# Adjacency build of a graph network: node groups of 17 in place of 16, their first edges counted exactly

## The chip, the cores and the metric

The kernel runs on one core of one Trainium2 chip. The metric is device time in microseconds (us) of one execution. TensorE is called PE in the profile, VectorE DVE, ScalarE ACT, GpSimd POOL, and SyncE, which here only issues transfers, SP.

## The reference, cut to what matters

Four graph layers run one after the other on 3,125 nodes with 96 features. All use the same 100,000 directed edges, whose `dst` is sorted:

```
_o = jnp.argsort(dst, stable=True)
src = src[_o]
dst = dst[_o]
...
msgs = xs[src]
agg = jax.ops.segment_sum(msgs, dst, num_segments=n_nodes)
...
x = x + _L0_gnn_ref(...)   # graph convolution, twice, batch norm between
x = x + _L1_gnn_ref(...)   # mean aggregation, twice
x = x + _L2_gnn_ref(...)   # attention over edges and self loops, twice
x = x + _L3_gnn_ref(...)   # normalized sum over edges
```

Every layer is preceded by a layer norm and a ReLU. The kernel gathers nothing edge by edge. It first builds the dense matrix of edge counts, source node by destination node, in 16 bit floats, and each `segment_sum` is then a matrix product with it.

## The kernel before

`build_adjacency` (L156) makes the matrix `adjacency` (`k.ADJ`). Its 3,125 destination columns are split into `NW` = 196 groups of `W` = 16 nodes. A source node is a row (`src & 127`, one of 128 partitions) and a tile (one of `NT` = 25). The edges of a group are a window of `WE` = 640 consecutive edges, that is `WT` = 5 batches of 128. A batch becomes two one-hot matrices: `hot_row` (edge by source row) and `hot_code` (edge by destination node within the group and source tile, a "code" out of 25 x 16 = 400). Their product on PE, summed over the five batches in PSUM (`counts`), is the group's part of the matrix. Since `dst` is sorted, batch b of a window holds only some of the group's nodes, and `RANGES` says which, so that the one-hot codes of a batch are narrower than 400. An edge that none of the ranges or windows reaches is found at the end by the total of the counts, and a slow loop over everything then runs (`sp.If(again)` and its like).

Four groups are a quad, and there are 49 quads. For each quad (`hot`, L349), DVE makes `hot_row` of all five batches with one instruction (L354) and `hot_code` of batches 0 to 3 with four instructions (L361). ACT makes the code of batch 4 out of a distance and a ReLU (L582, L590). PE multiplies (`pair`, L475: two groups, 16 matmuls, L486; three pairs of PSUM banks rotate), and ACT copies the counts of each pair into `adjacency` (L604). A matmul pair on each stored pair sums the out-degrees (L496).

Windows are loaded in eight loads (`LOADS`) of 4 to 36 groups, one transfer of two rows (`edge_keys`: row and code of each edge) per group, from an address that a register holds (L147, L152). SP issues nearly all of them, ACT a few of the first three loads. PE transposes a load's keys (`turn`, L470), and DVE unpacks them (`unpack`, L340, L341, L346).

The start addresses come first. Before the change, DVE takes every 25th edge of `dst` (32 samples in each of 125 partitions, L309, L311), compares each sample's group with all 196 group numbers (`below`, four instructions of 1,568 elements, L322), and PE sums the results over partitions and samples (32 matmuls of 196 columns, L456). 25 times the count (L330) is an address at most 25 edges ahead of the group's first edge. Five `bn_stats` of the first layer norm (L331) stand before L330, 20 behind it. Between the comparisons stands other work that the keys need: row and tile of each source (L313, L314), `dst_scaled` by ACT (L553) and the code (L317). SP and ACT write both keys to DRAM (L257, L558). The window transfers wait for those writes and for L330.

PE also runs matmuls whose results nobody reads, `keep_busy` (L449): 60 before the counting and 45 behind it, each `NW` columns wide. They stand in PE's queue ahead of the first `turn`.

The order of work on each engine is the order in which the code is written. Engines wait for each other by semaphores.

Of the kernel before, what the change touches and what calls it, by code (L numbers as in the profile page):

```python
# [13 lines left out]
I32 = mybir.dt.int32  # L14
# [18 lines left out]
W = 16  # L33
# [3 lines left out]
STEP = 25  # L37
NS = EF // STEP
SLICES = 4
LEAD = STEP  # L40
KEYS = LEAD + E + WE
CODES = NT * W
HALF = 0.5
RANGES = ((0, 6), (2, 10), (5, 15), (9, 16), (12, 16))
# [3 lines left out]
          for (lo, hi), seen in zip(RANGES, (0, 6, 10, 15, 16))]  # L48
QUAD = 4
ADDRESSES = 12  # L50
LOADS = (4, 8, 16, 24, 36, 36, 36, 36)
# [6 lines left out]
STATS_FIRST = 5  # L58
# [84 lines left out]
def load_windows(nc, k, d, eng, engine, load, keys, windows, landed):  # L143

    for at in range(0, len(windows), ADDRESSES):
        some = windows[at:at + ADDRESSES]
        _, starts = nc.values_load_multi_w_load_instructions(  # L147
            k.start_i[0:1, some[0]:some[-1] + 1], engines=[engine], min_val=0, max_val=STEP * EP * NS,
            skip_runtime_bounds_check_because="a start is STEP times a count of at most EP * NS samples")
        for w, start in zip(some, starts):  # L150
            i = w - FIRST[load]
            eng.dma_start(keys[2 * i:2 * i + 2, load % 2, :], d.keys[:, bass.ds(start, WE)]).then_inc(landed, 16)  # L152


def build_adjacency(nc, k, d, c):

    def sb(name, shape, dt):
        return c.enter_context(nc.sbuf_tensor(name, shape, dt))
# [20 lines left out]
    sample_i = sb("sample_i", [P, NS], I32)  # L179
    sample = sb("sample", [P, NS, 2], F16)  # L180
# [9 lines left out]
    below = [k.ADJ[0:EP, 7 + s, 0:NS // SLICES * NW] for s in range(SLICES)]  # L190
    pads = k.ADJ[0:1, 7 + SLICES, 0:4 * (LEAD + WE)].bitcast(F32).rearrange("p (e n) -> p e n", e=2)
# [14 lines left out]
    stats_ready = sem("stats_ready")  # L206
# [11 lines left out]
    key_writes = 16 * 6  # L218
# [24 lines left out]
    @block.sync  # L243
    def _(sp):
        for part, array in zip((dst[0:EVEN, :], dst[EVEN:EP, :]), pieces(d.dst)):
            sp.dma_start(part, array).then_inc(dst_in, 16)
        sp.wait_ge(pads_ready, 3)
        sp.dma_start(d.keys[:, 0:LEAD], pads[:, :, 0:LEAD]).then_inc(keys_out, 16)
        sp.dma_start(d.keys[:, LEAD + E:KEYS], pads[:, :, LEAD:LEAD + WE]).then_inc(keys_out, 16)
# [6 lines left out]
        for part, array in zip((code_f[0:EVEN, :], code_f[EVEN:EP, :]), pieces(d.keys[1, LEAD:LEAD + E])):  # L256
# [12 lines left out]
        again = sp.value_load(missed, min_val=0, max_val=1)  # L269
        with sp.If(again):  # L270
            sp.dma_start(g_row_f, d.keys[0, LEAD:LEAD + E].rearrange("(p f) -> p f", p=EP)).then_inc(g_keys_in, 16)
            sp.dma_start(g_code, d.keys[1, LEAD:LEAD + E].rearrange("(p f) -> p f", p=EP)).then_inc(g_keys_in, 16)
            sp.wait_ge(g_keys_in, 32)

    @block.gpsimd
    def _(pool):
# [6 lines left out]
        pool.iota(own[:, :], pattern=[[CODES // 2 * QUAD, MOST // QUAD], [0, WT], [CODES // 2, QUAD]], base=0,  # L283
# [10 lines left out]
        pool.memset(zeros[:, :], 0.0).then_inc(idents, 1)  # L294

    @block.vector
    def _(dve):
# [3 lines left out]
        dve.memset(pads[:, 1, 0:LEAD], -1.0).then_inc(pads_ready, 1)  # L301
        dve.memset(pads[:, 1, LEAD:], HALF * NT * (N + P)).then_inc(pads_ready, 1)
# [6 lines left out]
        chain(dve.tensor_scalar(sample_i[0:EP, :], dst.rearrange("p (s j) -> p s j", j=STEP)[:, :, 0], 4, None,  # L309
                                ALU.logical_shift_right))  # L310
        chain(dve.tensor_copy(sample[0:EP, :, :], sample_i[0:EP, :].unsqueeze(2).to_broadcast([EP, NS, 2])))  # L311
# [6 lines left out]
                                       op1=ALU.add).then_inc(codes_ready, 1)  # L318
        dve.wait_ge(iotas, 1)
        n = NS // SLICES  # L320
        for s in range(SLICES):
            dve.tensor_tensor(below[s].rearrange("p (s a b) -> p s a b", s=n, b=2),  # L322
                              bound[0:EP, :].rearrange("p (a b) -> p a b", b=2).unsqueeze(1).to_broadcast([EP, n, NW // 2, 2]),
                              sample[0:EP, s * n:(s + 1) * n, :].unsqueeze(2).to_broadcast([EP, n, NW // 2, 2]),
                              ALU.is_gt).then_inc(below_ready, 1)
        dve.wait_ge(x_in, 16 * (NG + 1))
        for t in range(NT):
            if t == STATS_FIRST:
                dve.wait_ge(count_ready, 1)
                dve.tensor_scalar(k.start_i[:, :], count_ps, float(STEP), None, ALU.mult).then_inc(starts_ready, 1)  # L330
            last = dve.bn_stats(node_stats[:, t, :], k.X[:, t, :])  # L331
        last.then_inc(stats_ready, 1)
        dve.wait_ge(iotas, 4)

# [14 lines left out]
        def hot(load, q):  # L349
# [94 lines left out]
    def _(pe):  # L444
        n = NS // SLICES
# [102 lines left out]
    def _(act):  # L548
# [8 lines left out]
        for part, array in zip((row_f[0:EVEN, :], row_f[EVEN:EP, :]), pieces(d.keys[0, LEAD:LEAD + E])):  # L557
            act.dma_start(array, part).then_inc(keys_out, 16)  # L558
# [16 lines left out]
        def distances(load, q):  # L575
# [4 lines left out]
            for w in range(QUAD):  # L580
                at = (q - quads(load)[0]) * QUAD + w
                nc.scalar.activation(distance[:, q % 2, w, :], codes_iota[:, FROM[-1]:CODES], ACT.Abs,  # L582
                                     bias=negative[:, load % 2, at:at + 1]).then_inc(distance_ready, 1)
# [1738 lines left out]
```

## Time and profile before

| | |
|---|---|
| time, median of 3 runs | 815.18 us (814.97 to 815.38) |
| span of the profiled execution, first to last instruction | 812.5 us |
| mean granted clock of PE | 0.953 of full |
| PE busy | 737.1 us (91%) |
| DVE busy | 605.8 us (75%) |
| ACT busy | 462.9 us (57%) |

No separate time of the profiled execution is given beyond its span. The median lies 2.7 us above the span, which is what lies around the first and last instruction. Shares of busy time are averages over stages with different limits. The adjacency build takes about the first 191 us, and only its rows bear on the change.

### The profile page before, as it was taken

The page shows a single profiled execution, that of the slowest core. Times are in us where ns is not written, and L with a number is a line of the kernel's source. Part 1 is how long each engine was busy: PE and PEld are TensorE (multiplying, and loading weights), DVE is VectorE, ACT ScalarE, POOL GpSimd, SP SyncE. Part 2 cuts the span into 40 slices and gives each one's busy share as a digit, 9 for nine tenths or more (in the row PEclk, how much of TensorE's full clock was granted, in tenths as well). Part 3 has the DMA queues.
Part 4 walks back from the last instruction along what each step waited for, and adds up shares of the span by engine and source line. Part 5 has one row for each costly group of instructions (what it writes and reads, how often), then busy time and mean ns, then how long its engine had stood idle before and what let it go on. Part 6 is the DMA issues. An engine that isn't in the chain of part 4 may idle for free. (4 is left out here: it accounts for less than half of the span.)

```text
span 812.5 us, 21039 instructions
## 1 busy us (share of the span) xinstructions
PE 737.1 (91%) x8477; PEld 681.0 (84%) x8477; DVE 605.8 (75%) x1376; ACT 462.9 (57%) x911; POOL 4.8 (1%) x15
## 2 busy tenths in 40 slices
PE   7888888888997999999999849999964999997997
PEld 6656666657997999999999839999964999997997
DVE  7999999997437445543444589999978999996732
ACT  2898898894004023212123668999656899973600
POOL 2000000000000000000000000000000000000000
PEclk9999999999999999999999979999965999998999
DMA  5000000001994000000000410776651099997801
GB/s 143 13 12 12 13 7 1 2 2 19 411 414 191 2 1 2 2 2 2 2 14 26 127 35 18 227 228 211 213 183 62 18 181 216 206 203 190 177 26 36
DMA packets 121660, 78.13 MB, mean 96 GB/s; under 512 B 98088, under 2 KB 116058, under 8 KB 121432
## 3 DMA queue, kind: packets, MB, share of 16 engines
q1 hardware_dynamic: 121216, 75.89, 33.2%
q8 instruction: 70, 1.15, 0.6%
q10 hardware_dynamic: 344, 0.85, 0.3%
q14 instruction: 30, 0.25, 0.1%
HBM read 30.46 MB, written 25.79 MB: 69 GB/s over the span
## 5 line engine op out<-in xcount | busy, mean ns | idle before, releaser
L1888 PE MATMUL banks<-loose,adjacency 128*128 128x194 f16 x1250 | 212.4, 247 | 0.0
L663 PE MATMUL banks<-y_sb,adjacency 128*128 128x192 f16 (+1 forms) x1875 | 165.9, 248 | 1.3 <-DVE h_sb L910 1.1
L663 PEld LDWEIGHTS banks<-y_sb,adjacency 128*128 128x128 f16 x1875 | 161.2, 99 | 2.2 <-DVE h_sb L910 1.3
L486 PEld LDWEIGHTS counts<-hot_code,hot_row 128*128 128x128 f16 x1568 | 92.8, 101 | 61.8 <-DVE hot_code L361 35.8
L1887 PE MATMUL banks<-x_sb,gat_masks 128*128 128x194 f16 x820 | 141.4, 248 | 1.9 <-DVE adjacency L1802 1.9
L486 PE MATMUL counts<-hot_code,hot_row 128*128 128x100 f16 (+3 forms) x1568 | 122.5, 218 | 20.0 <-DVE hot_code L361 14.9
L1858 ACT ACTIVATE gat_masks<-y_sb,node_scalars 128x640 bf16<-128x640 f32 x164 | 121.9, 827 | 4.0 <-PEq L117 4.0
L1888 PEld LDWEIGHTS banks<-loose,adjacency 128*128 128x128 f16 x1250 | 122.6, 98 | 0.3
L361 DVE TENSOR_TENSOR hot_code<-codes_iota,unpacked 128x600 f16<-128x600 f16 x196 | 96.8, 554 | 0.0
L604 ACT ACTIVATE adjacency<-counts 128x800 f16<-128x800 f32 x98 | 81.5, 832 | 18.0 <-PE counts L486 18.0
L1887 PEld LDWEIGHTS banks<-x_sb,gat_masks 128*128 128x128 f16 x820 | 80.4, 98 | 3.1 <-DVE y_sb L1798 2.4
L354 DVE TENSOR_TENSOR hot_row<-rows_iota,unpacked 128x2560 f16<-128x2560 f16 x49 | 72.5, 1479 | 0.0
L1141 ACT ACTIVATE y_sb<-banks 96x256 f32<-96x256 f32 x50 | 19.1, 382 | 93.6 <-PE banks L1173 93.6
L1798 DVE TENSOR_TENSOR gat_masks<-gat_masks,adjacency 128x1920 f16<-128x1920 bf16 (+1 forms) x64 | 64.2, 1005 | 6.7 <-ACT gat_masks L1858 6.4
L582 ACT ACTIVATE distance<-codes_iota,negative 128x100 f16<-128x100 f16 x196 | 57.6, 370 | 13.3 <-DVE negative L346 13.3
L1802 DVE TENSOR_TENSOR adjacency<-adjacency,gat_masks 128x1920 f16<-128x1920 f16 (+1 forms) x64 | 63.9, 1006 | 0.4
L692 DVE TENSOR_REDUCE h_sb<-banks 128x96 f32<-128x192 f32 x50 | 17.8, 356 | 57.0 <-PE banks L663 56.4
L692 DVE TENSOR_REDUCE y_sb<-banks 128x96 f32<-128x192 f32 x50 | 17.7, 355 | 52.5 <-PE banks L663 52.5
L663 PE MATMUL banks<-loose,adjacency 128*128 128x192 f16 x625 | 55.7, 246 | 0.0
L663 PEld LDWEIGHTS banks<-loose,adjacency 128*128 128x128 f16 x625 | 52.7, 99 | 0.0
L2160 PE MATMUL banks<-y_sb,adjacency 128*128 128x192 f16 x625 | 52.3, 245 | 0.2 <-DVE y_sb L2080 0.2
L2160 PEld LDWEIGHTS banks<-y_sb,adjacency 128*128 128x128 f16 x625 | 52.1, 97 | 0.3 <-issue 0.3
(236 smaller groups left out, 1008.4 us busy)
## 6 DMA issues: line engine op xcount, KB each, us to landing
kept_adj<-adjacency SPq DMA_DIRECT2D x5, 4000.0 KB, 30.4
adjacency<-kept_adj SPq DMA_DIRECT2D x25, 800.0 KB, 9.0
y_sb<-a_dst_rows SPq DMA_DIRECT2D x10, 320.0 KB, 4.0
window_keys<-edge_keys SPq DMA_DIRECT2D x187, 5.0 KB
residual<-h_sb SPq DMA_DIRECT2D x5, 240.0 KB, 2.0
kept_x<-x_sb SPq DMA_DIRECT2D x1, 1200.0 KB, 5.2
loose<-residual SPq DMA_DIRECT2D x5, 240.0 KB, 3.6
x_sb<-kept_x SPq DMA_DIRECT2D x5, 240.0 KB, 4.9
```

Of the source, the lines that this page charges most:

```text
L354: dve.tensor_tensor(hot_row[:, h, :, :].rearrange("p n (a b) -> p n a b", b=2), rows_iota[:, :].rearrange("p (a b) -> p a b", b=2).unsquee ...
L361: dve.tensor_tensor(hot_codes(h, b).rearrange("p w (a b) -> p w a b", b=2), codes_iota[:, FROM[b]:FROM[b] + WIDE[b]].rearrange("p (a b) -> ...
L486: last = nc.tensor.matmul(counts[:, 2 * (p % HELD) + i, start:end], hot_row[:, q % 2, b * QUAD + w, :], hot_codes(q % 2, b)[:, w, start - ...
L582: nc.scalar.activation(distance[:, q % 2, w, :], codes_iota[:, FROM[-1]:CODES], ACT.Abs, bias=negative[:, load % 2, at:at + 1]).then_inc(d ...
L604: nc.scalar.activation(k.ADJ[:, :, 2 * p * W:2 * (p + 1) * W].rearrange("p t (b o) -> p t b o", o=W), counts_of(2 * (p % HELD), 2), ACT.Co ...
L663: return nc.tensor.matmul(k.ps[:, j % G, 0:cols], k.ADJ[:, i, j * P:(j + 1) * P], y[:, i, 0:cols], start=i == 0, stop=i == NT - 1)
L1798: dve.tensor_tensor(masks(u, F16), masks(u, mybir.dt.bfloat16), counts_of(u), ALU.min).then_inc(t.over_ready, 1)
L1802: dve.tensor_tensor(counts_of(u), counts_of(u), masks(u, F16), ALU.subtract).then_inc(t.under_ready, 1)
L1858: nc.scalar.activation(step_of(x), row[ch % 2], ACT.Relu, bias=k.a_s5[:, i:i + 1], scale=STEEP).then_inc(t.step_ready, 1)
L1887: nc.tensor.matmul(bank[:, 0:2 * BC], over_of(x)[:, q * P:(q + 1) * P], features[0][:, i, :], start=i == 0, stop=False)
L1888: return nc.tensor.matmul(bank[:, 2 * BC:4 * BC], under_of(x)[:, q * P:(q + 1) * P], features[1][:, i, :], start=False, stop=i == NT - 1)
L2160: return nc.tensor.matmul(sums(j), k.ADJ[:, a * G + i % G, at:at + P], k.Y[:, i, 0:ONE], start=i == 0 and j % 2 == 0, stop=i == NT - 1 and ...
```

## The change

Groups have 17 nodes instead of 16, so there are 184 groups and 46 quads. A quad's ranges change, and its five widths go from 150, 200, 250, 176, 100 to 150, 200, 226, 200, 100 codes. `hot_code` now always compares with the start of `codes_iota`, and the offset of the range goes into `own`, which POOL prepares with five more instructions.

The first edge of a group is now counted exactly. A partition holds 800 consecutive edges, which touch at most three groups: that of its first edge (`dst * 241 >> 12`, which is the division by 17) and the next two. Two comparisons over the 800 edges, each with a running sum (`accum_out`), tell how many edges lie in or behind the second and the third. Three masks of 184 groups, multiplied with the numbers of edges in each, replace the 32 samples, and PE adds them up with three matmuls. The comparisons read `dst_scaled` and stand behind the code (L317 of before). Two `bn_stats` instead of five stand before the start addresses. The 25 pad keys ahead of the edges and their transfer go.

```
-W = 16
+W = 17
-STEP = 25
-NS = EF // STEP
-SLICES = 4
-LEAD = STEP
-KEYS = LEAD + E + WE
+DIVIDE, SHIFT = 241, 12
+SPAN = 3
+KEYS = E + WE
-RANGES = ((0, 6), (2, 10), (5, 15), (9, 16), (12, 16))
+RANGES = ((0, 6), (2, 10), (6, 15), (9, 17), (13, 17))
-LOADS = (4, 8, 16, 24, 36, 36, 36, 36)
+LOADS = (4, 8, 16, 24, 36, 36, 36, 24)
-STATS_FIRST = 5
+STATS_FIRST = 2
...
-        sp.dma_start(d.keys[:, 0:LEAD], pads[:, :, 0:LEAD]).then_inc(keys_out, 16)
...
+        pool.wait_ge(iotas, 4)
+        by_batch = own[:, :].rearrange("p (g b w) -> p g b w", b=WT, w=QUAD)
+        for b in range(WT):
+            pool.tensor_scalar(by_batch[:, :, b, :], by_batch[:, :, b, :], HALF, HALF * FROM[b], ALU.mult,
+                               ALU.add).then_inc(own_ready, 1)
...
-        chain(dve.tensor_scalar(sample_i[0:EP, :], dst.rearrange("p (s j) -> p s j", j=STEP)[:, :, 0], 4, None,
-                                ALU.logical_shift_right))
-        chain(dve.tensor_copy(sample[0:EP, :, :], sample_i[0:EP, :].unsqueeze(2).to_broadcast([EP, NS, 2])))
+        chain(dve.tensor_scalar(base_i[0:EP, :], dst[:, 0:1], DIVIDE, None, ALU.mult))
+        chain(dve.tensor_scalar(base_i[0:EP, :], base_i[0:EP, :], SHIFT, None, ALU.logical_shift_right))
+        for r in range(SPAN):
+            chain.later(dve.tensor_scalar(bases[0:EP, r:r + 1], base_i[0:EP, :], float(r), None, ALU.add))
+            chain.later(dve.tensor_scalar(edges[0:EP, r:r + 1], base_i[0:EP, :], float(r), HALF * NT * W, ALU.add, ALU.mult))
...
+        for r in range(1, SPAN):
+            chain.later(dve.tensor_scalar(later[:, r, :], dst_scaled, edges[0:EP, r:r + 1], None, ALU.is_ge, ALU.add,
+                                          accum_out=beyond[0:EP, r:r + 1]))
+        chain.all()
+        chain.later(dve.tensor_scalar(within[0:EP, 0:1], beyond[0:EP, 1:2], -1.0, float(EF), ALU.mult, ALU.add))
+        chain.later(dve.tensor_copy(within[0:EP, 2:3], beyond[0:EP, 2:3]))
+        chain(dve.tensor_tensor(within[0:EP, 1:2], beyond[0:EP, 1:2], beyond[0:EP, 2:3], ALU.subtract))
         dve.wait_ge(iotas, 1)
-        n = NS // SLICES
-        for s in range(SLICES):
-            dve.tensor_tensor(below[s].rearrange("p (s a b) -> p s a b", s=n, b=2),
-                              ...
-                              ALU.is_gt).then_inc(below_ready, 1)
+        for r in range(SPAN):
+            dve.tensor_scalar(below[:, r, :], bound[0:EP, :], bases[0:EP, r:r + 1], within[0:EP, r:r + 1], ALU.is_gt,
+                              ALU.mult).then_inc(below_ready, 1)
...
-                                  codes_iota[:, FROM[b]:FROM[b] + WIDE[b]].rearrange("p (a b) -> p a b", b=2).unsqueeze(1)
+                                  codes_iota[:, 0:WIDE[b]].rearrange("p (a b) -> p a b", b=2).unsqueeze(1)
...
-        for s in range(SLICES):
-            pe.wait_ge(below_ready, s + 1)
-            for i in range(n):
-                last = nc.tensor.matmul(count_ps, k.ones_h[0:EP, 0:1], below[s][:, i * NW:(i + 1) * NW],
-                                        start=s == 0 and i == 0, stop=s == SLICES - 1 and i == n - 1)
+        for r in range(SPAN):
+            pe.wait_ge(below_ready, r + 1)
+            last = nc.tensor.matmul(count_ps, k.ones_h[0:EP, 0:1], below[:, r, :], start=r == 0, stop=r == SPAN - 1)
```

DVE from the landing of `dst` to the start addresses, as it was (x is a repeat count; the 1,568 wide comparisons are the samples'):

```order
L309 TENSOR_SCALAR sample_i<-adjacency 125x32
L311 CAST sample<-sample_i 125x64
L313 TENSOR_SCALAR adjacency<-adjacency 125x800
L314 TENSOR_SCALAR adjacency<-adjacency 125x800
L317 SCALAR_TENSOR_TENSOR adjacency<-adjacency 125x800
L322 TENSOR_TENSOR adjacency<-bound,sample 125x1568 x4
L331 BN_STATS node_stats<-x_sb 128x6 x5
L330 TENSOR_SCALAR start_i<-degree_ps 1x196
```

The same stretch of DVE now, without the six one-element instructions that follow `base_i` (line numbers are those of the changed kernel):

```order
L313 TENSOR_SCALAR base_i<-base_i 125x1
L318 TENSOR_SCALAR adjacency<-adjacency 125x800
L319 TENSOR_SCALAR adjacency<-adjacency 125x800
L322 SCALAR_TENSOR_TENSOR adjacency<-adjacency 125x800
L325 TENSOR_SCALAR adjacency,beyond<-adjacency,edges 125x800 x2
L328 TENSOR_SCALAR within<-beyond 125x1
L329 COPY within<-beyond 125x1
L330 TENSOR_TENSOR within<-beyond 125x1
L333 TENSOR_SCALAR adjacency<-bound,bases,within 125x184 x3
L340 BN_STATS node_stats<-x_sb 128x6 x2
L339 TENSOR_SCALAR start_i<-degree_ps 1x184
```

Eight one-element instructions now stand ahead of the row and tile of the sources. The first mask can only start when all comparisons are done.

PE from its first instruction to the first quad, before:

```order
L449 MATMUL keys_ps<-bound 128x196 x60
L456 MATMUL degree_ps<-adjacency,ones_h 1x196 x32
L449 MATMUL keys_ps<-bound 128x196 x45
L470 MATMUL keys_ps<-ident,window_keys 128x8 x5
L470 MATMUL keys_ps<-ident,window_keys 128x2x8 x5
```

And now:

```order
L458 MATMUL keys_ps<-bound 128x184 x60
L464 MATMUL degree_ps<-adjacency,ones_h 1x184 x3
L458 MATMUL keys_ps<-bound 128x184 x45
L477 MATMUL keys_ps<-ident,window_keys 128x8 x5
L477 MATMUL keys_ps<-ident,window_keys 128x2x8 x5
```

The numbers of filling matmuls stay, each 12 columns narrower. Of the 32 counting matmuls between them three are left.

## Rows read from the trace of the kernel before

**Rows 1.** The page: busy time, share and instructions of each engine.

```profile
PE 737.1 (91%) x8477; PEld 681.0 (84%) x8477; DVE 605.8 (75%) x1376; ACT 462.9 (57%) x911; POOL 4.8 (1%) x15
```

**Rows 2.** Timeline, DVE (start us, us, engine line op names shapes).

```profile
39.01 0.41 DVE L340 CAST unpacked<-keys_ps 128x240 f16<-128x240 f32 x1
39.85 1.49 DVE L354 TENSOR_TENSOR hot_row<-rows_iota,unpacked 128x2560 f16<-128x2560 f16 x1
...
121.11 0.52 DVE L340 CAST unpacked<-keys_ps 128x360 f16<-128x360 f32 x1
122.21 1.48 DVE L354 TENSOR_TENSOR hot_row<-rows_iota,unpacked 128x2560 f16<-128x2560 f16 x1
...
162.84 1.48 DVE L354 TENSOR_TENSOR hot_row<-rows_iota,unpacked 128x2560 f16<-128x2560 f16 x1
166.13 1.48 DVE L354 TENSOR_TENSOR hot_row<-rows_iota,unpacked 128x2560 f16<-128x2560 f16 x1
...
185.90 0.19 DVE L375 TENSOR_TENSOR mean<-node_stats 128x25 f32<-128x25 f32 x1
```

**Rows 3.** Lines by form, 0 to 200 us (count | busy us, mean ns | idle before).

```profile
L361 DVE TENSOR_TENSOR hot_code<-codes_iota,unpacked 128x1000 f16<-128x1000 f16 x49 | 33.0, 673 | 0.0
L361 DVE TENSOR_TENSOR hot_code<-codes_iota,unpacked 128x600 f16<-128x600 f16 x49 | 22.6, 461 | 0.0
```

**Rows 4.** Timeline, ACT, one quad in the loop.

```profile
179.93 0.84 ACT L604 ACTIVATE adjacency<-counts 128x800 f16<-128x800 f32 x1 [0.24 <-PE counts L486]
180.66 0.53 ACT L590 ACTIVATE hot_code<-distance 128x400 f16<-128x400 f16 x1
181.09 0.83 ACT L604 ACTIVATE adjacency<-counts 128x800 f16<-128x800 f32 x1
```

**Rows 5.** Waits, 12 to 200 us (us in total, times, longest).

```profile
PEld counts L486 <- DVE hot_code L361: 35.8, 123, 0.4
```

**Rows 6.** Timeline, DVE, from the first memsets to the first quad.

```profile
2.32 0.06 DVE L304 MEMSET ones_h<- 128x2 f16 x1
...
6.28 0.19 DVE L309 TENSOR_SCALAR sample_i<-adjacency 125x32 int32<-125x32 int32 x1 [2.66 <-DMA adjacency<-in_dst]
...
6.73 0.58 DVE L313 TENSOR_SCALAR adjacency<-adjacency 125x800 int32<-125x800 int32 x1
7.23 0.57 DVE L314 TENSOR_SCALAR adjacency<-adjacency 125x800 int32<-125x800 int32 x1
7.83 0.99 DVE L317 SCALAR_TENSOR_TENSOR adjacency<-adjacency 125x800 f32<-125x800 int32 x1
8.74 3.62 DVE L322 TENSOR_TENSOR adjacency<-bound,sample 125x1568 f16<-125x1568 f16 x4
12.28 0.89 DVE L331 BATCH_NORM_STATS2 node_stats<-x_sb 128x6 f32<-128x96 f32 x5
13.29 0.35 DVE L330 TENSOR_SCALAR start_i<-degree_ps 1x196 int32<-1x196 f32 x1
...
17.66 0.20 DVE L340 CAST unpacked<-keys_ps 128x40 f16<-128x40 f32 x1 [0.82 <-PE keys_ps L470]
```

**Rows 7.** Timeline, PE, the same stretch.

```profile
1.20 7.69 PE L449 MATMUL keys_ps<-bound 128*128 128x196 f16 x60 [1.20 <-POOL bound L278]
9.76 3.50 PE L456 MATMUL degree_ps<-adjacency,ones_h 125*1 125x196 f16 x32 [0.88 <-DVE adjacency L322]
13.19 3.96 PE L449 MATMUL keys_ps<-bound 128*128 128x196 f16 x45
17.08 0.47 PE L470 MATMUL keys_ps<-ident,window_keys 8*128 8x8 f32 x5
```

**Rows 8.** Busy time by window (engines, PEclk, DMA share, GB/s).

```profile
16.57:19.98 3.41, 1.46 (x17) 1.11 (x15) 2.56 (x8) 1.69 (x5) 0.00 (x0) 1.00 0.06 16
19.98:23.40 3.42, 3.27 (x32) 2.66 (x32) 3.38 (x8) 1.45 (x6) 0.00 (x0) 0.50 0.07 18
23.40:26.81 3.41, 2.75 (x39) 1.94 (x37) 3.41 (x6) 3.41 (x9) 0.00 (x0) 1.00 0.03 7
```

More of the change, by code:

```diff
@@ L47 @@
 PIECES = [[(lo * NT, min(hi, seen) * NT), (max(lo, seen) * NT, hi * NT)] if lo < seen < hi else [(lo * NT, hi * NT)]
-          for (lo, hi), seen in zip(RANGES, (0, 6, 10, 15, 16))]
+          for (lo, hi), seen in zip(RANGES, (0, 6, 10, 15, 17))]
 QUAD = 4
 ADDRESSES = 12
-LOADS = (4, 8, 16, 24, 36, 36, 36, 36)
+LOADS = (4, 8, 16, 24, 36, 36, 36, 24)
 FIRST = [sum(LOADS[:n]) for n in range(len(LOADS) + 1)]
@@ L147, in load_windows @@
         _, starts = nc.values_load_multi_w_load_instructions(
-            k.start_i[0:1, some[0]:some[-1] + 1], engines=[engine], min_val=0, max_val=STEP * EP * NS,
-            skip_runtime_bounds_check_because="a start is STEP times a count of at most EP * NS samples")
+            k.start_i[0:1, some[0]:some[-1] + 1], engines=[engine], min_val=0, max_val=E,
+            skip_runtime_bounds_check_because="a start is a count of at most E edges")
         for w, start in zip(some, starts):
@@ L178, in build_adjacency @@
     per_edge = sb("per_edge", [P, P], F16)
-    sample_i = sb("sample_i", [P, NS], I32)
-    sample = sb("sample", [P, NS, 2], F16)
+    base_i = sb("base_i", [P, 1], I32)
+    bases, edges = sb("bases", [P, SPAN], F32), sb("edges", [P, SPAN], F32)
+    beyond, within = sb("beyond", [P, SPAN], F32), sb("within", [P, SPAN], F32)
     total = sb("total", [1, 1], F32)
@@ L189, in build_adjacency @@
     dst_scaled, row_f, code_f = (early(t, F32, EF) for t in range(4, 7))
-    below = [k.ADJ[0:EP, 7 + s, 0:NS // SLICES * NW] for s in range(SLICES)]
-    pads = k.ADJ[0:1, 7 + SLICES, 0:4 * (LEAD + WE)].bitcast(F32).rearrange("p (e n) -> p e n", e=2)
+    below = k.ADJ[0:EP, 7, 0:SPAN * NW].rearrange("p (r w) -> p r w", r=SPAN)
+    later = k.ADJ[0:EP, 8, 0:SPAN * EF].rearrange("p (r f) -> p r f", r=SPAN)
+    pads = k.ADJ[0:1, 9, 0:4 * WE].bitcast(F32).rearrange("p (e n) -> p e n", e=2)
     counts = c.enter_context(nc.psum_tensor("counts", [P, 2 * HELD, 512], F32))
@@ L246, in _ @@
             sp.dma_start(part, array).then_inc(dst_in, 16)
-        sp.wait_ge(pads_ready, 3)
-        sp.dma_start(d.keys[:, 0:LEAD], pads[:, :, 0:LEAD]).then_inc(keys_out, 16)
-        sp.dma_start(d.keys[:, LEAD + E:KEYS], pads[:, :, LEAD:LEAD + WE]).then_inc(keys_out, 16)
+        sp.wait_ge(pads_ready, 2)
+        sp.dma_start(d.keys[:, E:KEYS], pads).then_inc(keys_out, 16)
         sp.wait_ge(x_pad, 1)
@@ L255, in _ @@
         sp.wait_ge(codes_ready, 1)
-        for part, array in zip((code_f[0:EVEN, :], code_f[EVEN:EP, :]), pieces(d.keys[1, LEAD:LEAD + E])):
+        for part, array in zip((code_f[0:EVEN, :], code_f[EVEN:EP, :]), pieces(d.keys[1, 0:E])):
             sp.dma_start(array, part).then_inc(keys_out, 16)
@@ L282, in _ @@
                            base=0, pattern=[[-1, P]], channel_multiplier=1).then_inc(idents, 1)
-        pool.iota(own[:, :], pattern=[[CODES // 2 * QUAD, MOST // QUAD], [0, WT], [CODES // 2, QUAD]], base=0,
+        pool.iota(own[:, :], pattern=[[CODES * QUAD, MOST // QUAD], [0, WT], [CODES, QUAD]], base=0,
                   channel_multiplier=0, allow_small_or_imprecise_dtypes=True).then_inc(iotas, 1)
@@ L300, in _ @@
         dve.memset(pads[:, 0, :], -1.0).then_inc(pads_ready, 1)
-        dve.memset(pads[:, 1, 0:LEAD], -1.0).then_inc(pads_ready, 1)
-        dve.memset(pads[:, 1, LEAD:], HALF * NT * (N + P)).then_inc(pads_ready, 1)
+        dve.memset(pads[:, 1, :], HALF * NT * (N + P)).then_inc(pads_ready, 1)
         dve.memset(k.X[:, NT - 1, :], 0.0).then_inc(x_pad, 1)
@@ L333, in _ @@
         dve.wait_ge(iotas, 4)
+        dve.wait_ge(own_ready, WT)
         def unpack(load):
@@ L556, in _ @@
         act.wait_ge(rows_f_ready, 1)
-        for part, array in zip((row_f[0:EVEN, :], row_f[EVEN:EP, :]), pieces(d.keys[0, LEAD:LEAD + E])):
+        for part, array in zip((row_f[0:EVEN, :], row_f[EVEN:EP, :]), pieces(d.keys[0, 0:E])):
             act.dma_start(array, part).then_inc(keys_out, 16)
@@ L581, in distances @@
                 at = (q - quads(load)[0]) * QUAD + w
-                nc.scalar.activation(distance[:, q % 2, w, :], codes_iota[:, FROM[-1]:CODES], ACT.Abs,
+                nc.scalar.activation(distance[:, q % 2, w, :], codes_iota[:, 0:WIDE[-1]], ACT.Abs,
                                      bias=negative[:, load % 2, at:at + 1]).then_inc(distance_ready, 1)
```

13 lines of the change are left out of this document (5 added, 8 removed).

## Prediction

> **What bounds the kernel now.** I read the page first, then the lines of the first 200 us by form, then the timeline of that stretch engine by engine. The page makes PE the busiest engine at 91% [rows 1], but that is an average. In the adjacency build it is DVE. One quad follows the other at 162.84, 166.13 us, so every 3.29 us, with no idle time before any of these rows [rows 2]. The lines by form say the same: no idle time before DVE's one-hot instructions [rows 3]. PE, on the other hand, waits for DVE's `hot_code` 123 times, 35.8 us in total [rows 5], and ACT still waits 0.24 us in a quad for counts of PE [rows 4]. So the loop's length is DVE's work, and DVE has it without a gap from the first unpack at 17.66 to the layer norm's L375 at 185.90 [rows 6, 2].
>
> What starts the loop is a chain in the first 17 us: `dst` lands (6.28), the keys are made, the samples are compared (8.74 to 12.36), PE counts (to 13.26), L330 at 13.29 gives the addresses [rows 6, 7]. The last step is different. The row of the first `turn` at 17.08 has no idle time before it, and the 45 filling matmuls in front of it ran from 13.19 to 17.15 [rows 7]. The windows had landed, so the end of the filling sets the start of the loop, and DVE waits for that turn (0.82 us before 17.66) [rows 6].
>
> **The loop: three quads fewer.** The five instructions of a quad on DVE keep their sum of elements. `hot_row` stays at 2,560. `hot_code` had 600 + 800 + 1,000 + 704 = 3,104, and now has 600 + 800 + 904 + 800 = 3,104. From 600 to 1,000 elements the duration goes from 461 to 673 ns, 0.53 ns per element [rows 3], so it is linear in what is moved around and a quad stays at 3.29 us. The 1,000 wide batch started at code 125, an odd 16 bit offset, and lies on the same line, so that starting at zero gains nothing. Three quads fewer are 3 x 3.29 = 9.88 us.
>
> Unpacking 36 groups takes DVE 122.21 - 121.11 = 1.10 us, 24 groups 39.85 - 39.01 = 0.84 us [rows 2]. The last load shrinks from 36 to 24: 0.26 us. Together 10.14 us of 168.24.
>
> **What rides along in the loop.** ACT stores 850 elements per pair instead of 800. From 400 to 800 its instructions go from 0.53 to 0.83 us [rows 4], 0.75 ns per element, so two stores are 0.08 us longer in a quad and lie inside the 0.24 us of waiting. PE's counting columns stay 875 per group, the degree matmuls get 25 more, 100 in a quad. That is about 0.04 us at the full level, under the 0.73 us per quad that it waits for DVE (35.8 / 49) [rows 5]. Nothing of both counts, until the end. The last stores and sums behind DVE's last quad are 6% wider, about 0.1 us. POOL's five instructions on `own` run some 10 us before the first unpack needs them. The narrower pads, and a transfer fewer on SP ahead of the loads of x, can help those by some tenths of a us. They end before DVE gets to `bn_stats` as it is (no idle time before 12.28 [rows 6]).
>
> **The start addresses.** Durations of one-element instructions are not in the trace of before in this place. Lower bound is 0.06 us (two elements, 2.32), upper 0.22 each if each waited for the one before (two dependent ones from 6.28 to 6.73 take 0.45) [rows 6]. The first two are chained, six are not: 2 x 0.21 + 6 x 0.09 = 0.96, of which 0.45 replaces the sample's two. So the key instructions slip by 0.5, and the code starts at 8.3 and is followed at 9.25. Each comparison has 800 elements. The int32 one of 7.23 is followed after 0.60 us, the f32 one of 7.83 after 0.91 [rows 6]. I take the latter, since the output is f32 with a sum beside it: 11.07, bounds 10.45 and 11.1. Waiting for both sums and three small ones adds 0.45: 11.5. The masks have 184 elements, between 0.11 (0.57 ns per element of L322, 3.62 / 6,272) and 0.3 each. With 0.2 they end at 12.1. Three matmuls of PE add 0.25 where the last eight took 0.9 (12.36 to 13.26), and L330's successor starts at 12.4, against 13.29. Gain 0.9 us, bounds 1.7 and 0 (other costs all high). The keys' transfers are issued 0.5 later, still before the addresses.
>
> VectorE: DVE Perf Modes, section "Two Vector instructions with no wait between them", of the Trainium skill says that an instruction that also writes its accumulator counts as two, the main one and a read of the accumulator. No row of before shows such an instruction. As an estimate from that page's rule, a second short instruction for each comparison would take away about 0.1 us of that gain, twice.
>
> **What PE does with it.** The gain reaches the loop only through the filling matmuls. At full clock 45 of them with 184 columns take 3.96 x 184 / 196 = 3.72 us [rows 7], from 12.4 to 16.1, and the turn would come 0.9 us earlier than 17.08. But look at the time before. The 60 first fillers end at 8.89, and PE then waited 0.88 us for the first quarter of the samples [rows 7]. Now the 60 are narrower, end near 8.6, and the first mask is ready near 11.7. PE stands idle for 3.1 us, and then does three small matmuls. The same happened in this trace later: with PE busy 1.46 of the 3.41 us from 16.57, the granted clock was 0.50 from 19.98 to 23.40 (1.2 in place of 2.4 GHz), and full again behind a busy stretch [rows 8]. I expect one such stretch at half level, of 3.41 us as in that row, most of it in the 45 fillers. At half level a filler takes twice the 0.083 us. If all 3.41 us fall in them they take 1.7 us longer, if 2.8 us do, 1.4. I take 1.4: 12.4 + 3.72 + 1.4 = 17.5, a turn 0.4 us later than before instead of 0.9 earlier. Bounds are 0.9 gained and 0.9 lost.
>
> TensorE: Matmul & The Clock Gate, section "What's actually happening", of the Trainium skill says that the clock's observation is free-running and not tied to a kernel's start, so that the moment of a change of level varies between runs. By it this term would be anything between the two bounds from one run to the next. The three times of before differ by 0.41 us, so this trace bears it out little.
>
> **The sum.** -10.14 (loop) + 0.1 (end) + 0.4 (start) = -9.6 us. Span 812.5 - 9.6 = 802.9 us. With the 2.7 us that the median has over the span, 815.18 - 9.6 = 805.6 us. What follows the build is the same program on the same matrix and moves forward as a whole. Only the stretches at half clock at its phase changes can fall differently, and each moves PE by up to half of 3.41 us. I put 1 us on both sides for all of them.
>
> **Rivals.**
> 1. The clock stays up in the prologue, or falls only outside the fillers. For it: PE gets some work at 12 us, and the first fillers ran until 8.6. Against: rows 8. Then the start gains 0.9: 815.18 - 10.14 + 0.1 - 0.9 = 804.2 us.
> 2. ACT becomes the bound and the kernel slower. A group is now 17 values, 34 bytes, so every second run in the store starts at no multiple of 4 bytes, and its reads are 25 apart in PSUM as before. The slack is 0.24 us per quad [rows 4]. A store longer by d makes a quad longer by 2d - 0.24. It decides from d = 0.12 on, and the saved 9.6 us are gone at 2d - 0.24 = 9.6 / 46 = 0.21, so d = 0.22 us (0.83 to 1.05). If the store took 1.5 times its time, d = 0.42, the quads get 0.60 longer and the kernel 46 x 0.60 = 27.6 slower than forecast: 833 us. Against: the store's duration goes by the element, and DVE's one-hot that reads from an odd 16 bit offset cost nothing more [rows 3].
> 3. Little comes through: PE's or SP's part of the loop becomes late (a window load that DVE then waits for), or the slow loop over all edges runs because a window or range is too small. SP has fewer windows to load per us of loop than before, and the average group has 544 edges of 640. A slow loop would cost more than everything else here together. Within 0.2% of before would need a loss of 8 us in the loop, 0.17 per quad, for which no row speaks.
> 4. The half level comes twice in the prologue, and a later phase loses a stretch too: up to 808.
>
> **How the numbers follow.** Forecast 805.6 us, chance 0.60. Rival 1 0.25 (804.2). Rival 4 0.09. Rival 2 0.03. Rival 3 0.03. The forecast's own range is 804.5 to 806.7. The range that holds 8 in 10 takes in rival 1 with 1 us of clock below it and a part of rival 4: 803.1 to 807.6. What can be told from no change is 0.2%, 1.6 us. All but rivals 2 and 3 are faster by more: faster 0.95, same 0.02, slower 0.03.
>
> **What would show it.** In the profile after: `hot_row` starts 3.29 us apart, no idle time on DVE in the loop, 46 of them, and 158.1 us from first unpack to L375's successor (right loop). A store of ACT near 0.87 us (0.95 or more makes ACT the bound). The comparisons start 0.91 apart (0.60: addresses at 11.8). A window of half clock between 12 and 17 us and a first turn at 17.5 (16.2: rival 1). The instruction of L375, at 185.90 before, at 176.2. It is wrong if a quad is longer than 3.3 us, or if the phases behind the build are not as long as they were to within 1 us.

## The result, and the profile after

| | before | after |
|---|---|---|
| median, us | 815.21 (814.97 to 815.38, 4 runs) | 804.91 (803.71 to 805.32, 4 runs) |
| span of the profiled execution, us | 812.5 | 803.2 |

The ratio is 0.9873, 95% interval 0.9859 to 0.9887. Forecast were 805.6 us and a range of 803.1 to 807.6, so the time is inside it and the direction right. The profiled execution after took 805.0 us, 1.8 more than its span. The 2.7 us put around the span of before, there and in the forecast, were not all of that kind: in every recorded run of before the time lies 2.2 to 2.4 us above the span, so some 0.4 us were the difference between that one execution and the median. The changed kernel has 1.8 in each of its four runs. So another 0.5 us of the gain lies outside the spans, where no row shows it.

The spans differ by 9.3 us. The steps, each from the two traces: first unpack 17.66 to 19.53, 1.9 later. Loop to the layer norm's first instruction 168.24 to 158.01, 10.2 shorter. From there to the first product of the next phase 7.92 to 8.08, 0.2 longer. The first product 20.90 to 19.28, 1.6 shorter. All behind it 0.5 longer.

The loop in the timeline of DVE after, against [rows 2, 6]:

```profile
19.53 0.20 DVE L350 CAST unpacked<-keys_ps 128x40 f16<-128x40 f32 x1 [2.73 <-PE keys_ps L477]
...
170.96 1.48 DVE L364 TENSOR_TENSOR hot_row<-rows_iota,unpacked 128x2560 f16<-128x2560 f16 x1
...
174.25 1.48 DVE L364 TENSOR_TENSOR hot_row<-rows_iota,unpacked 128x2560 f16<-128x2560 f16 x1
...
177.54 0.19 DVE L385 TENSOR_TENSOR mean<-node_stats 128x25 f32<-128x25 f32 x1
```

Quads follow after 3.29 us as before, and 46 of them take the place of 49. The lines by form of the first 200 us show why a quad costs the same, against [rows 3]:

```profile
L371 DVE TENSOR_TENSOR hot_code<-codes_iota,unpacked 128x800 f16<-128x800 f16 x92 | 51.8, 563 | 0.0
L371 DVE TENSOR_TENSOR hot_code<-codes_iota,unpacked 128x904 f16<-128x904 f16 x46 | 28.4, 617 | 0.0
L371 DVE TENSOR_TENSOR hot_code<-codes_iota,unpacked 128x600 f16<-128x600 f16 x46 | 21.1, 459 | 0.0
```

459 + 2 x 563 + 617 = 2,202 ns, and no idle time before any. Before, the four widths that a quad had then (those of [rows 3] and the two below) sum to 461 + 565 + 673 + 515 = 2,214 ns:

```profile
L361 DVE TENSOR_TENSOR hot_code<-codes_iota,unpacked 128x800 f16<-128x800 f16 x49 | 27.7, 565 | 0.0
L361 DVE TENSOR_TENSOR hot_code<-codes_iota,unpacked 128x704 f16<-128x704 f16 x49 | 25.3, 515 | 0.0
```

ACT, one quad of the loop, against [rows 4]:

```profile
171.57 0.88 ACT L611 ACTIVATE adjacency<-counts 128x850 f16<-128x850 f32 x1 [0.15 <-PE counts L493]
172.35 0.53 ACT L597 ACTIVATE hot_code<-distance 128x400 f16<-128x400 f16 x1
172.78 0.87 ACT L611 ACTIVATE adjacency<-counts 128x850 f16<-128x850 f32 x1
```

The store takes 0.87 us as worked out (0.83 us + 50 x 0.75 ns), and ACT's wait shrank from 0.24 to 0.15 us. The means over all stores, 832 and 876 ns, differ by 44 ns where 38 were worked out, so the odd groups of 17 cost next to nothing of their own.

The start, timeline of DVE after, against [rows 6]:

```profile
6.46 0.15 DVE L312 TENSOR_SCALAR base_i<-adjacency 125x1 int32<-125x1 int32 x1 [2.81 <-DMA adjacency<-in_dst]
...
7.22 0.56 DVE L318 TENSOR_SCALAR adjacency<-adjacency 125x800 int32<-125x800 int32 x1
...
9.21 1.04 DVE L325 TENSOR_SCALAR_CACHE_REDUCE adjacency<-adjacency,edges 125x800 f16<-125x800 f32 x1
...
10.17 0.08 DVE L325 DVE_READ_ACCUMULATOR adjacency<-adjacency,edges 125x1 f32 x1
10.17 1.04 DVE L325 TENSOR_SCALAR_CACHE_REDUCE adjacency<-adjacency,edges 125x800 f16<-125x800 f32 x1
...
11.57 0.80 DVE L333 TENSOR_SCALAR adjacency<-bound,bases,within 125x184 f16<-125x184 f16 x3
...
12.78 0.34 DVE L339 TENSOR_SCALAR start_i<-degree_ps 1x184 int32<-1x184 f32 x1
```

The addresses come 0.5 us earlier than before, 6.3 us behind the landing of `dst` instead of 7.0. PE after, against [rows 7]:

```profile
1.19 6.45 PE L458 MATMUL keys_ps<-bound 128*128 128x184 f16 x60 [1.19 <-POOL bound L277]
11.96 0.79 PE L464 MATMUL degree_ps<-adjacency,ones_h 125*1 125x184 f16 x3 [4.31 <-DVE adjacency L333]
12.68 6.31 PE L458 MATMUL keys_ps<-bound 128*128 128x184 f16 x45
18.92 0.47 PE L477 MATMUL keys_ps<-ident,window_keys 8*128 8x8 f32 x5
```

PE waited 4.31 us for the first mask, and the 45 fillers then took 6.31 us instead of 3.96. Busy time by window, against [rows 8]:

```profile
8.21:11.62 3.41, 0.00 (x0) 0.00 (x0) 3.31 (x10) 0.47 (x1) 0.00 (x0) 0.94 0.88 266
11.63:18.46 6.83, 6.50 (x44) 5.94 (x45) 5.09 (x29) 0.00 (x0) 0.00 (x0) 0.53 0.12 37
```

The granted clock was at half for 6.8 us, from about 11.2 to 18.0 (it is full again in the last 0.4 us of the second row), over most of the fillers. The last pair of rows is the first product, 225 matmuls, before and after:

```profile
193.82 20.90 PE L663 MATMUL banks<-y_sb,adjacency 128*128 128x193 f16 x225 [0.21 <-DVE y_sb L710]
```

```profile
185.62 19.28 PE L670 MATMUL banks<-y_sb,adjacency 128*128 128x193 f16 x225 [0.21 <-DVE y_sb L717]
```

In the trace of before a stretch of 3.41 us at half clock lay on it:

```profile
194.06:197.48 3.42, 3.42 (x24) 3.19 (x22) 3.35 (x7) 1.21 (x2) 0.00 (x0) 0.50 0.29 45
```

Nothing in the change touches this product. The experiments look at whose 1.6 us these are.

### The profile page after: what moved, and what is told of

It is laid out like the page before. It is cut to its first block and busy times, and to the rows that moved or that the text cites. A ratio compares the mean times of both kernels' runs of the same rounds, so it can differ in the third digit from the quotient of the medians.

```text
span 803.2 us, 20695 instructions
## 1 busy us (share of the span) xinstructions
PE 723.5 (90%) x8340; PEld 667.5 (83%) x8340; DVE 595.8 (74%) x1372; ACT 458.3 (57%) x890; POOL 6.0 (1%) x20
## 5 line engine op out<-in xcount | busy, mean ns | idle before, releaser
L493 PEld LDWEIGHTS counts<-hot_code,hot_row 128*128 128x128 f16 x1472 | 81.7, 98 | 64.4 <-DVE hot_code L371 39.3
L493 PE MATMUL counts<-hot_code,hot_row 128*128 128x150 f16 (+1 forms) x1472 | 111.9, 215 | 22.1 <-DVE hot_code L371 12.8
L371 DVE TENSOR_TENSOR hot_code<-codes_iota,unpacked 128x800 f16<-128x800 f16 (+2 forms) x184 | 90.6, 550 | 0.0
L611 ACT ACTIVATE adjacency<-counts 128x850 f16<-128x850 f32 x92 | 80.6, 876 | 12.8 <-PE counts L493 12.4
L364 DVE TENSOR_TENSOR hot_row<-rows_iota,unpacked 128x2560 f16<-128x2560 f16 x46 | 68.1, 1480 | 0.0
L589 ACT ACTIVATE distance<-codes_iota,negative 128x100 f16<-128x100 f16 x184 | 54.1, 372 | 14.3 <-DVE negative L356 14.3
```

The lines of the kernel that those rows point to most:

```text
L364: dve.tensor_tensor(hot_row[:, h, :, :].rearrange("p n (a b) -> p n a b", b=2), rows_iota[:, :].rearrange("p (a b) -> p a b", b=2).unsquee ...
L493: last = nc.tensor.matmul(counts[:, 2 * (p % HELD) + i, start:end], hot_row[:, q % 2, b * QUAD + w, :], hot_codes(q % 2, b)[:, w, start - ...
L611: nc.scalar.activation(k.ADJ[:, :, 2 * p * W:2 * (p + 1) * W].rearrange("p t (b o) -> p t b o", o=W), counts_of(2 * (p % HELD), 2), ACT.Co ...
```

## The experiments

Ten experiments ran, in three sets, each set on a chip of its own and with its own runs of before: medians 814.48 (813.48 to 816.18, 17 runs), 815.11 (813.26 to 817.03, 17 runs), 814.85 (813.28 to 816.21, 9 runs). The same kernel thus spreads over some 3 us, more than the first four runs of before had shown. The table has what the traces say of the start and the loop (us, filler counts in brackets); the two kernels with narrower ranges come at the end of this section.

| kernel | addresses | fillers behind the counting | first turn | first unpack | loop | median |
|---|---|---|---|---|---|---|
| before | 13.29 | 3.96 (45) | 17.08 | 17.66 | 168.24 | 815.21 |
| after | 12.78 | 6.31 (45) | 18.92 | 19.53 | 158.01 | 804.91 |
| after again | 12.21 | 4.81 (45) | 16.85 | 17.46 | 158.02 | 803.61 |
| 100 first fillers | 12.35 | 3.74 (45) | 17.85 | 18.42 | 158.10 | 804.42 |
| 20 fillers | 12.14 | 2.42 (20) | 15.81 | 16.62 | 158.06 | 803.07 |
| 90 fillers | 12.22 | 7.30 (90) | 19.34 | 19.95 | 158.89 | 807.84 |
| exact counting, 16 nodes | 12.19 | 3.96 (45) | 15.98 | 16.59 | 168.19 | 815.63 |
| samples, 17 nodes | 12.83 | 3.73 (45) | 16.39 | 16.99 | 158.13 | 804.42 |
| samples, 17 nodes, 20 fillers | 13.04 | 1.76 (20) | 16.62 | 17.29 | 158.05 | 804.16 |
| before, 20 fillers | 14.12 | 2.19 (20) | 17.69 | 18.24 | 168.19 | 814.48 |

Two things have to be known to read this table. `dst` landed at 5.74 to 6.46 us in these ten traces, so the starts differ by up to 0.7 us before the counting has begun. Counted from the landing, the addresses come after 6.3 us with exact counting in all six traces of it, and after 7.0 to 7.1 us with the samples (8.1 in the last row). And what lies behind the first product of the next phase, the same program in all, took between 597.8 and 599.7 us from trace to trace. A start that is 1 or 2 us better can be lost in that.

### Which half of the change does it

Groups of 17 alone (the samples put back, `dst * 241 >> 12` for 32 samples in place of the shift by 4):

```
-        for r in range(1, SPAN):
-            chain.later(dve.tensor_scalar(later[:, r, :], dst_scaled, edges..., accum_out=beyond...))
+        for s in range(SLICES):
+            dve.tensor_tensor(below[s]..., bound..., sample..., ALU.is_gt).then_inc(below_ready, 1)
```

> Groups of 17 nodes alone, with the samples of before (one more small instruction on DVE for the division by 17). Theory A: PE has no long gap, fillers take 3.7 to 3.9 us, first unpack at 17.9, loop of 158.0 us as in the changed kernel. Counted from before 815.2 - 10.1 + 0.1 + 0.2 = 805.4 us, counted from the changed kernel 804.9 - 1.6 = 803.3 us. The two differ by the stretch at half clock in the first product, which before had (20.9 us for 225 matmuls) and the changed kernel had not (19.3 us): whichever it shows, its time is to follow. Rival D: with the old counting it is slower than the changed kernel, 805.4 or more, whatever the first product shows.

Measured 804.42 us (802.85 to 805.12), ratio 0.9870, interval 0.9853 to 0.9888. The loop was 158.13 us as expected. The trace had the stretch at half clock on the first product (20.60 us), for which 805.4 was expected, and this execution took 804.61: what the first product shows does not fix the time to 1 us.

Exact counting alone:

```
-W = 17                              +W = 16
-DIVIDE, SHIFT = 241, 12             +DIVIDE, SHIFT = 1, 4
```

(with the ranges and loads of before)

> Exact counting alone, with groups of 16 nodes as before (49 quads, ranges and loads of before). Theory A: the loop is as long as before (168.2 us), the first unpack comes at 19.5 instead of 17.7 because of the fillers, time 815.2 + 1.9 = 817.1 us, give or take 1 for stretches at half clock in later phases. Rival D (the new counting gains by itself, since its addresses come 0.5 us earlier): 814.7 us.

Measured 815.63 us (812.61 to 817.18, 12 runs), ratio 1.0009, interval 0.9999 to 1.0018. So the gain is the 17 nodes. The counting gives nothing that can be measured. The 817.1 expected did not come, but a loss is not excluded: the median is 1.2 us above the 814.48 of before in its set, and the interval allows up to 0.18%. The loop stays at 168.19 us here, although `hot_code` starts at zero and the offset is in `own`, so that part of the change gives the loop nothing.

Time minus span is 1.7 to 1.9 us in all runs of this kernel and of that with the samples and 17 nodes, against 2.2 to 2.4 in all runs of before, with 45 fillers or with 20. What these two kernels share is POOL's preparation of `own` and the codes that start at zero; no run separates that further.

The profiled run did not show the slow fillers that I expected. PE waited only 2.47 us for the first mask and the clock stayed up. This execution, 812.61 us, was the fastest of the twelve, 3.0 us below their median, and what the others had there is not known:

```profile
1.20 7.75 PE L458 MATMUL keys_ps<-bound 128*128 128x196 f16 x60 [1.20 <-POOL bound L277]
11.43 0.73 PE L464 MATMUL degree_ps<-adjacency,ones_h 125*1 125x196 f16 x3 [2.47 <-DVE adjacency L333]
12.09 3.96 PE L458 MATMUL keys_ps<-bound 128*128 128x196 f16 x45
```

### What sets the start of the loop

```
-BUSY_FIRST, BUSY_NEXT, BUSY_TAIL = 60, 45, 10
+BUSY_FIRST, BUSY_NEXT, BUSY_TAIL = 100, 45, 10     # first kernel
+BUSY_FIRST, BUSY_NEXT, BUSY_TAIL = 60, 20, 10      # second
+BUSY_FIRST, BUSY_NEXT, BUSY_TAIL = 60, 90, 10      # third
```

> The changed kernel with 100 instead of 60 filling matmuls ahead of the counting, so that PE has work until the first mask is nearly ready. Theory A (PE's idle time from 7.6 to 12.0 us lowers its clock, and the 45 fillers behind the counting then take 6.3 us and hold the first turn until 18.9): granted clock 1.0 from 12 to 16 us, fillers take 3.7 us, first turn at about 16.6, first unpack at 17.0 (bn_stats end at 16.8) instead of 19.5, time 804.9 - 2.5 = 802.4 us. Rival B (the window transfers or something else behind the addresses hold the turn): first turn stays at 18.9, time 804.9. If the 40 more matmuls run at half level to the end, the counting slips by up to 0.9 us and the gain is 1.6.

The clock did stay up and the fillers took 3.74 us, as theory A has it. The turn was still late, at 17.85, because of something else in this execution: SP waited 1.9 us for a write of the keys before it could send the window transfers, and PE 1.87 us for them.

```profile
SPq L145 <- DMA edge_keys<-adjacency: 1.9, 1, 1.9
```

```profile
11.91 0.40 PE L464 MATMUL degree_ps<-adjacency,ones_h 125*1 125x184 f16 x3
12.24 3.74 PE L458 MATMUL keys_ps<-bound 128*128 128x184 f16 x45
17.85 0.44 PE L477 MATMUL keys_ps<-ident,window_keys 8*128 8x8 f32 x5 [1.87 <-DMA window_keys<-edge_keys]
```

Median 804.42 us (802.57 to 805.30), ratio 0.9872 (0.9854 to 0.9891): the 2.5 us did not come.

> The changed kernel with 20 instead of 45 filling matmuls behind the counting; the clock is left as low as it falls. Theory A: 20 fillers at half level take 2.8 us, end at 15.5, the windows land at about 16.3, first turn at 16.5, first unpack at 17.0, time 804.9 - 2.5 = 802.4 us, at a low clock in the first quads, which costs nothing since DVE bounds them. Rival B: turn stays at 18.9, 804.9 us. Rival C (the low clock itself costs in the first quads, not the fillers' length): between 803.5 and 804.9.

Median 803.07 us (802.39 to 804.28), ratio 0.9861 (0.9845 to 0.9878). In its trace the clock was at half from 13.0 us, the fillers were over at 14.45, the turn came at 15.81 behind a wait for the windows (1.36 us), and DVE waited only 0.47 us. In that trace the start is 2.9 us earlier than in the first trace after, of which 0.6 us is the earlier landing of `dst`. Whether the median is better can't be told: the intervals overlap.

> The changed kernel with 90 instead of 45 filling matmuls behind the counting. If the fillers set the start of the loop, 45 more at 0.083 us (full level again by then) put the first turn 3.7 us later than in the changed kernel with the clock as it falls: first unpack at 21 to 23, time 804.9 + 3.7 = 808.6 us, or somewhat less where the windows were the later ones. If windows or the layer norm set it: unchanged, 804.9 us.

Median 807.84 us (807.36 to 809.31), ratio 0.9917 (0.9900 to 0.9933), against 803.61 for the unchanged kernel in the same set: 4.2 us longer, 3.7 expected. Against the trace of the unchanged kernel in that set the first unpack comes 2.5 us later, and the loop is 0.9 us longer, of which 0.76 is a wait of DVE for the third load's keys (at 31.58). So the fillers set the start where they outlast the windows. This is the one dose that stands clear of the spread.

> Groups of 17 with the samples of before, and 20 fillers instead of 45. In the trace of the same kernel with 45 the first turn came at 16.39 with no idle time before it and DVE waited 0.63 us. With 20 the windows (addresses at 13.1, transfers from 14.15) land at about 16.2 and set the turn: gain 0.2 to 0.6 us, 804.4 - 0.4 = 804.0 us. Against the exact counting with 20 fillers (803.1) the samples should be about 0.5 us later in their addresses: slower by 0.5, within what the runs spread.

Median 804.16 us (803.29 to 805.06), ratio 0.9870 (0.9851 to 0.9889). The windows set the turn (PE waits 1.93 us for them), at 16.62 in this trace and not earlier than with 45. A difference to 804.42 can't be told.

> The kernel before with 20 instead of 45 fillers behind the counting. Its turn at 17.08 had no idle time before it. With 20 the windows set it, at about 16.7: DVE's 0.82 us of waiting falls to 0.4, time 815.2 - 0.4 = 814.8 us. If fillers matter by keeping the clock up for the first quads, it would be slower than before by up to 1 us; DVE bounds those quads, so I expect none of that.

Median 814.48 us (813.18 to 815.67, 11 runs), ratio 0.9995 (0.9985 to 1.0006). The expected 0.4 us can be neither shown nor excluded. The windows did set the turn (PE waits 1.49 us for them), but the addresses were 0.8 us later than before, so the trace doesn't say how near the fillers were to being the bound in the old kernel. It shows a second thing: with the samples too the clock can fall in front of the counting. The 32 counting matmuls took 4.54 us instead of 3.50, DVE waited 1.17 us for them, and the addresses came at 14.12. The granted clock was at half from about 11.3 to 14.7 us, behind a wait of only 1.54 us for the first samples.

### The changed kernel once more

> The changed kernel once more, unchanged. Theory P (how PE's slow stretches fall differs from run to run, and with it where the loop starts): the first trace had half level from 11.6 to 18.5 us and 6.3 us of fillers. This one should differ there, fillers between 3.7 and 6.3 us, first unpack between 17 and 19.5, and the runs should spread over about 2 us around 804. Rival Q (the half level behind the counting is fixed by the kernel): 6.3 us again, first unpack 19.5. Loop from first unpack to the layer norm 158.0 us under both.

Median 803.61 us (802.40 to 804.32), ratio 0.9853 (0.9837 to 0.9868). The same program had half level for 3.4 us here, not 6.8, and its fillers took 4.81 us:

```profile
11.39 0.79 PE L464 MATMUL degree_ps<-adjacency,ones_h 125*1 125x184 f16 x3 [3.87 <-DVE adjacency L333]
12.11 4.81 PE L458 MATMUL keys_ps<-bound 128*128 128x184 f16 x45
16.85 0.47 PE L477 MATMUL keys_ps<-ident,window_keys 8*128 8x8 f32 x5
```

The first unpack came at 17.46, which is 0.2 us earlier than in the trace of before instead of 1.9 later. (`dst` landed 0.4 us earlier than in that trace, so counted from there it is 0.2 later.) Theory P holds: where the slow stretches fall is a matter of the execution. The 2.1 us between the two first unpacks of this program left only 0.7 in the spans (803.2 and 802.5). The first product took 19.28 us in every trace but two, that of before (20.90) and that of the samples with 17 nodes (20.60). The kernel before with 20 fillers has 19.28 too. So the 1.6 us go with no part of the change.

### Does DVE alone bound the loop

```
-RANGES = ((0, 6), (2, 10), (6, 15), (9, 17), (13, 17))
+RANGES = ((0, 5), (3, 10), (6, 14), (10, 17), (13, 17))   # DVE's batches
+RANGES = ((0, 5), (3, 10), (6, 14), (10, 17), (14, 17))   # ACT's batch too, and BUSY_NEXT = 20
```

> The changed kernel with narrower ranges for batches 0 to 3 (5, 7, 8, 7 nodes instead of 6, 8, 9, 8). They are the narrowest that these inputs allow, the slow loop being there for others. DVE's hot_code falls from 3,104 to 2,712 elements, 392 x 0.53 ns = 0.21 us per quad. If DVE alone bounds the loop: quads of 3.08 us, 9.6 us less. If ACT is as near as its waits say (0.16 us per quad left in the changed kernel's trace): ACT becomes the bound, quads of 3.13 us, loop 158.0 - 7.4 = 150.6 us, time 804.3 - 7.4 = 796.9 us, with small waits of DVE or PE for ACT. If something else held the quads at 3.29 us: no change.

Median 796.56 us (793.51 to 797.26), ratio 0.9765 (0.9741 to 0.9789), loop 19.20 to 169.02 = 149.8 us. Quads follow after 3.09 us. In the quads shown ACT has no waits left, each of its instructions follows on the last:

```profile
140.98 0.89 ACT L611 ACTIVATE adjacency<-counts 128x850 f16<-128x850 f32 x1
141.75 0.53 ACT L597 ACTIVATE hot_code<-distance 128x400 f16<-128x400 f16 x1
142.18 0.87 ACT L611 ACTIVATE adjacency<-counts 128x850 f16<-128x850 f32 x1
142.94 1.17 ACT L589 ACTIVATE distance<-codes_iota,negative 128x100 f16<-128x100 f16 x4
144.07 0.88 ACT L611 ACTIVATE adjacency<-counts 128x850 f16<-128x850 f32 x1
```

DVE has one wait in this whole loop, 1.04 us for the third load's keys. The median is near the 796.9 that I had put down for ACT as the bound, but for another reason: the first unpack came late, at 19.20.

> As the one with narrower ranges on DVE, and ACT's batch 4 narrowed too (3 nodes instead of 4: four distances of 75 elements, a ReLU of 304, 0.75 ns per element, 0.14 us less per quad), and 20 fillers behind the counting instead of 45. ACT then needs 2.99 us, DVE 3.08, so DVE bounds again: loop 158.0 - 9.6 = 148.4 us, first unpack at about 17, time 803.1 - 9.6 = 793.5 us. If PE becomes the bound, it shows quads over 3.1 us and DVE waiting for counts.

Median 794.51 us (794.17 to 796.31), ratio 0.9761 (0.9744 to 0.9778), loop 149.7 us, quads again 3.09 us:

```profile
160.16 1.48 DVE L364 TENSOR_TENSOR hot_row<-rows_iota,unpacked 128x2560 f16<-128x2560 f16 x1
163.25 1.49 DVE L364 TENSOR_TENSOR hot_row<-rows_iota,unpacked 128x2560 f16<-128x2560 f16 x1
166.34 0.20 DVE L385 TENSOR_TENSOR mean<-node_stats 128x25 f32<-128x25 f32 x1
```

ACT was given some 0.14 us per quad by the estimate, its idle time before the stores rose from 5.9 to 11.4 us in total, and the quads did not get shorter. So DVE bounds both, and ACT in the first of them had only just run out of slack. DVE's price per element is confirmed (0.20 us less per quad for 392 elements, 0.21 expected). The loop was 1.3 us longer than the 148.4 expected. Of this 0.95 us is one wait of DVE for the third load's keys (at 27.82), which DVE reached before PE had turned them. These ranges are meant to be the narrowest that the given inputs allow; no run tries narrower ones. For other inputs the slow loop would stand in. With that proviso both versions beat both kernels. Between the two the medians can't tell: the intervals overlap.

## Why the prediction was right or wrong

**The loop, -10.14 us: right,** measured -10.23, and 158.0 to 158.1 in six traces of groups of 17 with these ranges and up to 45 fillers. Both parts of it held: the quad at 3.29 us, and the smaller last load. That the sum of DVE's elements stays was the step on which all rested. The forecast called the price linear on two widths, which any two would allow; the 800 and 704 wide rows of before, 565 and 515 ns, are what shows it. The 704 wide batch starts at code 225, also an odd 16 bit offset, so an odd offset cost nothing in either.

**What rides along: right.** ACT kept 0.15 of 0.24 us. Its price of 0.75 ns per element came from two different instructions (a ReLU of 400, a store of 800). Between the two stores, 800 and 850 wide, it is 0.88, and the difference is too small to matter. The tail cost 0.16 us for 0.1 forecast.

**The addresses, 0.9 us earlier (bounds 1.7 and 0): within the bounds.** They came 0.5 earlier, 0.7 counted from the landing of `dst`. The small instructions went faster than thought (6.46 to 7.22, 0.76 for 0.96), the comparisons slower (0.96 us from one to the next for 0.91), and PE's three matmuls ran at half level (0.79 us where the kernel with 100 fillers took 0.40). I had taken the comparisons' output for f32. It is f16, and they were no faster than the price taken. What the Trainium skill says of accumulator outputs (VectorE: DVE Perf Modes, section "Two Vector instructions with no wait between them"), that such an instruction is two, the main one and a read of the accumulator, agrees with this trace: each comparison is followed by an instruction that reads the accumulator, 0.08 us long. A comparison with its read cost 0.05 us more than the price taken, half of the estimate.

**What PE does with it, +0.4 us with bounds of 0.9 on both sides: the step that failed.** In this trace the mechanism was the one described: PE idles, its clock falls, and the fillers hold the turn. "One such stretch at half level, of 3.41 us" was the mis-sized part. There were 6.8 us of it, the fillers took 6.3 us, and the start lost 1.9 us, twice the bound. PE's idle time was mis-sized too, 4.3 us for 3.1: the 60 first fillers ended at 7.64 and not at 8.6 (they took 6.3 to 7.7 us in the traces of this and the other kernels with 17 nodes, though the rows give full level for all of them). Nor is the loss a property of the kernel. The unchanged kernel once more had its first unpack no later than before, and a wait of 2.5 us for the first mask left the clock up (exact counting with 16 nodes). The rule of the Trainium skill that I had set aside, that the observation is free-running and not tied to a kernel's start (TensorE: Matmul & The Clock Gate, section "What's actually happening"), agrees with these runs: 6.31 and 4.81 us for the same 45 matmuls in two executions of one program. The small spread of the first runs of before (0.4 us) was no evidence against it. Later runs of before spread over 3.8.

**The sum, 805.6 for 804.91.** The span was forecast at 802.9 us and was 803.2. In the profiled run a start worse by 1.5 us was made up by the first product, which here had no slow stretch (1.6), with 0.5 given back later: the errors cancelled by chance. The phases behind the build were 0.94 us shorter in all, just inside the 1 us that the forecast allowed, though the first product alone was outside it. Above the span the forecast had 2.7 us and there were 1.8, which made up the rest. What of the total is steady is the loop, and the 0.5 us outside the spans, for which the forecast had no term and no run has the cause. What the rest of it contributes lies within the spread.

**Rivals.** Rival 2 (ACT becomes the bound) is refuted by the stores of 0.87 us, and the narrowed ranges show how near it lay: 0.2 us less of DVE per quad and ACT's slack is gone. Rival 1 (clock stays up) describes single executions, not the kernel. Rival 3 (little comes through) did not come. Rival 4 came by half: 6.8 us are its two stretches in the prologue, but the later phases lost none beyond what before lost, so the time was not near 808. The length of PE's wait ahead of the counting doesn't decide by itself what the clock does there: it fell behind waits of 1.54, 2.90 and 3.85 to 4.31 us and stayed up behind 1.50, 2.47 and 2.54. What does decide is not settled by these traces.

## What to carry to other kernels

When one engine bounds a loop, count its elements per trip before and after: here a bigger group with the same number of elements was a gain of exactly the trips that fell away. Matmuls that only keep PE busy stand in its queue, so compare their end, at either level of the clock, with when the data lands: 90 of them cost 4.2 us here, and whether 20 are better than 45 could not be told. Before a gain of a microsecond is credited to a part, run the same program again and look at whether the part's rows repeat. Compare the profiled execution with the median of its kernel: here one was 3 us off.

## What the runs showed of the hardware

- The same instructions of one program ran with half level for 6.8 us in one execution and 3.4 in another, and the runs of before spread over up to 3.8 us of 815. No run says how much of that spread is the clock's.
- A comparison of 800 f32 elements with a running sum and an f16 output takes 1.04 us, and a read of the accumulator of 0.08 us follows; an int32 operation of 800 without a sum takes 0.56. They differ in type and in the sum, and no run separates the two.
- DVE's one-hot comparisons from a table that starts at an odd 16 bit offset (codes 125 and 225) took 673 ns at 1,000 elements and 515 at 704, on one line with 461 at 600 and 565 at 800 from even offsets.
- A write of keys landed late enough in one execution to hold the transfers behind it by 1.9 us, though the DMA engines were busy 8% or less of the time from 12 us on.
- A store of ACT of 850 16 bit values in runs of 17 took 876 ns in the mean, one of 800 in runs of 16 took 832.
